# Another order of work in the cached attention stage of a four-part block

## The reference, cut to what matters

```
h = layernorm(x)
q, k_new, v_new = h @ wq.T, h @ wk.T, h @ wv.T
k = concat(k_cache, k_new);  v = concat(v_cache, v_new)      # 1601 cached + 256 new keys
x = x + (softmax(q @ k.T / 16) @ v) @ wo.T
```

## Time and profile before

| | |
|---|---|
| median of three runs | 1695.53 us |
| the profiled execution, its own time | 1699.32 us |
| its span, first to last instruction | 1697.5 us |
| PE busy over the span | 1455.1 us (86%) |
| DVE, ACT, POOL busy over the span | 1160.9, 984.3, 568.0 us |
| mean granted PE clock over the span | 0.94 |
| cached attention: first to last instruction | 0 to 199.13 us |
| PE busy in 0 to 199.2 us | 143.88 us (granted clock 0.89) |
| DVE, ACT, POOL busy in it | 90.08, 83.19, 49.76 us |

### The profile page before, as it was taken

One profiled execution on the slowest core, in us unless ns is written; L12 is line 12 of the kernel. 1 busy time (PEld: TensorE's weight loads), 2 busy tenths in 40 slices (PEclk: granted clock), 3 DMA queues, 4 the chain that ended last, 5 costly groups with the idle time before them and its releaser, 6 DMA issues. The chain is left out here.

```text
span 1697.5 us, 27527 instructions
## 1 busy us (share of the span) xinstructions
PE 1455.1 (86%) x10079; PEld 1363.0 (80%) x10082; DVE 1160.9 (68%) x2329; ACT 984.3 (58%) x2062; POOL 568.0 (33%) x470
## 2 busy tenths in 40 slices
PE   5778547888858989899999989999989999999945
PEld 4677546877747989899999989999989999999823
DVE  4553466888856777667676766777766677777657
ACT  3445216787735656566666566665656656666535
POOL 2223313453244522343223343233324333322134
PEclk8988857999979999999999999999999999999968
DMA  5132118889812302011011110110201101000010
GB/s 190 64 115 102 35 60 278 293 292 321 269 56 53 80 4 68 20 39 41 7 41 44 31 50 9 40 41 8 68 20 38 42 8 41 20 8 23 26 50 25
DMA packets 83547, 128.05 MB, mean 75 GB/s; under 512 B 17108, under 2 KB 63352, under 8 KB 83032
## 3 DMA queue, kind: packets, MB, share of 16 engines
q1 hardware_dynamic: 78856, 113.84, 20.8%
q0 software_dynamic: 4560, 12.46, 2.8%
HBM read 114.28 MB, written 11.99 MB: 74 GB/s over the span
## 5 line engine op out<-in xcount | busy, mean ns | idle before, releaser
L1843 ACT ACTIVATE ga_pT<-ga_ps_t 128x512 fp32r<-128x512 f32 (+1 forms) x512 | 243.7, 516 | 255.0 <-PE ga_ps_t L2077 254.7
L1978 DVE TENSOR_TENSOR ga_pT<-ga_ps_t,ga_pT 128x512 fp32r<-128x512 f32 (+1 forms) x512 | 280.2, 583 | 95.7 <-ACT ga_pT L1843 93.6
L1851 ACT ACTIVATE ga_probs<-ga_ps_s,ga_neg_max 128x1200 f32<-128x1200 f32 (+1 forms) x256 | 235.5, 927 | 91.8 <-DVE ga_neg_max L1999 91.4
L2077 PE MATMUL ga_ps_t<-all_eye,ga_probs 128*128 128x128 f32 (+1 forms) x1664 | 227.0, 274 | 9.7 <-DVE ga_pT L1978 9.6
L2077 PEld LDWEIGHTS ga_ps_t<-all_eye,ga_probs 128*128 128x128 f32 (+1 forms) x1664 | 193.0, 141 | 19.6 <-DVE ga_pT L1978 12.4
L1994 DVE TENSOR_REDUCE ga_part_max<-ga_ps_s 128x1 f32<-128x1200 f32 x128 | 178.8, 1397 | 12.4 <-PE ga_ps_s L2028 11.1
L1745 POOL TENSOR_TENSOR ga_oT<-ga_out_n,ga_oT 128x256 fp32r<-128x256 f32 x64 | 47.5, 742 | 394.8 <-ACT ga_oT L1866 394.8
L2028 PE MATMUL ga_ps_m<-ga_pT,ga_v 128*128 128x256 f32 (+1 forms) x1248 | 174.1, 287 | 3.3 <-DVE ga_pT L1978 3.2
L2028 PE MATMUL ga_ps_m<-ga_pT,side_v 128*128 128x256 f32 (+1 forms) x1248 | 174.8, 287 | 0.5 <-DVE ga_pT L1978 0.3
L2028 PE MATMUL ga_ps_t<-side_w_kv,side_encT 128*128 128x256 f32 (+1 forms) x1170 | 162.2, 288 | 13.7 <-DVE ga_pT L1978 8.4
L2028 PEld LDWEIGHTS ga_ps_t<-side_w_kv,side_encT 128*128 128x128 f32 (+1 forms) x1170 | 144.8, 186 | 23.2 <-DVE ga_pT L1978 11.2
(11 more groups left out here) (293 smaller groups left out, 2649.3 us busy)
## 6 DMA issues: line engine op xcount, KB each, us to landing
ex_raw<-in_L_ffn_packed SPq DMA_DIRECT2D x63, 704.0 KB, 5.8
side_w_q_raw<-in_L_xattn_Wq SPq DMA_DIRECT2D x16, 512.0 KB, 4.9
side_w_q_raw<-in_L_xattn_Wo SPq DMA_DIRECT2D x16, 512.0 KB, 4.6
ga_inv_rows<-ga_inv_row SPq DMA_DIRECT2D x64, 128.0 KB, 3.0
mix_y_rows<-ex_y SPq DMA_DIRECT2D x63, 128.0 KB, 4.1
side_enc<-in_ctx_turned SPq DMA_DIRECT2D x12, 512.0 KB, 5.6
ca_keys<-in_ctx_turned SPq DMA_DIRECT2D x12, 464.0 KB, 6.7
ca_cache<-in_ctx SPq DMA_DIRECT2D x4, 1024.0 KB, 5.5
```

Source lines behind the costliest of these rows:

```text
L1843: nc.scalar.activation(dst(HI), src, ACT.Copy, scale=scale).then_inc(read, 1)
L1851: nc.scalar.activation(dst, src, ACT.Exp, bias=neg_max[:, n % 2:n % 2 + 1], accum_out=half_sum[:, n % 4, k:k + 1]).then_inc(exped, 1)
L1978: nc.vector.tensor_tensor(dst(LO), src, f32(dst(HI)), ALU.subtract).then_inc(empty, 1)
L2077: mm = nc.tensor.transpose(out[0:top, i * P:(i + 1) * P], probs[step % PB][:, tile * P:tile * P + top], eye[:, :])
```

## The change

Work of the cached attention is moved between steps; no arithmetic is added or removed. DRAIN goes from 3 to 4.

- xT of row b+1 goes from the odd step 2b+1 to the end of the even step 2b. The norm of row b+1 goes from the end of that even step to its head on DVE, ahead of `invert` and `largest`.
- v of row 0 goes from step 2 to step 0. The other v keep their step.
- y of row b-2 goes from the even step to the odd step after it (on PE behind the first two turns; `add` on DVE behind those turns).
- f and `ternary_scale` of matrix b-1 go from the even step to the end of the odd step; `ternary_sum` from the middle to the end of the even step on ACT; `ternary_sign` from the end of the odd step to the middle of the next even step.
- The cached values are split in three pieces of 4, 4 and 5 tiles, all three in the even step, on ACT and on POOL. The weigh pieces wait for the piece that they need.
- In the odd step, q stands between the first and the second `keys_high`. In the prologue ACT does xT ahead of the keys and the weights K ahead of the third piece of keys.
- On SP the next keys are issued ahead of the first half of the cached values.

```diff
-    halves = [range(0, 8), range(8, KT)]
+    thirds = [range(0, 4), range(4, 8), range(8, KT)]
...
         if t:
             to = b + 1
-            xT, q, k = ([(kind, 0, to)] if to < B else [] for kind in ("xT", "q", "k"))
-            return first + turns[0:2] + xT + values[0:1] + q + turns[2:3] + k + values[1:2] + turns[3:4]
-        v = [("v", 0, b - 1)] if 0 <= b - 1 < B else []
-        y = [("y", 0, b - 2)] if 0 <= b - 2 < B else []
-        f = [("f", 0, b - 1)] if 0 <= b - 1 < W else []
-        return first + turns[0:2] + values[0:1] + turns[2:3] + values[1:2] + turns[3:4] + v + y + f
+            q, k = ([(kind, 0, to)] if to < B else [] for kind in ("q", "k"))
+            y = [("y", 0, b - 2)] if 0 <= b - 2 < B else []
+            f = [("f", 0, b - 1)] if 0 <= b - 1 < W else []
+            return first + turns[0:2] + y + values[0:1] + q + turns[2:3] + k + values[1:2] + turns[3:4] + f
+        v = [("v", 0, row) for row in ((0,) if b == 0 else (b - 1,) if 1 <= b - 1 < B else ())]
+        xT = [("xT", 0, b + 1)] if b + 1 < B else []
+        return first + turns[0:2] + values[0:1] + turns[2:3] + values[1:2] + turns[3:4] + v + xT
...
@@ SyncE
             for b in range(1, B):
-                load_cache(b, 0)
                 if b + 1 < B:
                     load_keys(b + 1)
+                load_cache(b, 0)
                 load_cache(b, 1)
...
@@ GpSimd
-                if 0 <= b - 1 < B:
-                    split_cache(b - 1, t)
+                if t == 0 and 0 <= b - 1 < B:
+                    for h in range(3):
+                        split_cache(b - 1, h)
...
@@ ScalarE, prologue
             weight_high(Q)
+            ring(("xT", 0, 0))
             keys_high(0, 0)
             keys_high(0, 1)
-            ring(("xT", 0, 0))
+            weight_high(K)
             keys_high(0, 2)
+            ring(("q", 0, 0))
             keys_high(0, 3)
-            weight_high(K)
-            ring(("q", 0, 0))
             ring(("k", 0, 0))
...
@@ ScalarE, odd step
-                        ring(("xT", 0, to))
                         keys_high(to, 0)
+                        ring(("q", 0, to))
                         keys_high(to, 1)
-                        ring(("q", 0, to))
...
-                    if 0 <= b - 1 < B:
-                        cache_high(b - 1, 1)
-                    if 0 <= b - 1 < W:
-                        ternary_sign(b - 1)
@@ ScalarE, even step
                 else:
+                    if b == 0:
+                        ring(("v", 0, 0))
                     if 0 <= b - 1 < B:
                         cache_high(b - 1, 0)
-                    if 0 <= b - 1 < W:
-                        ternary_sum(b - 1)
                     for e in turns[2:3]:
                         ring(e)
                     if 0 <= b - 2 < B:
                         result_high(b - 2)
                     for e in turns[3:4]:
                         ring(e)
+                    if 0 <= b - 2 < W:
+                        ternary_sign(b - 2)
                     if 0 <= b - 1 < B:
+                        cache_high(b - 1, 1)
+                    if 1 <= b - 1 < B:
                         ring(("v", 0, b - 1))
+                    if b + 1 < B:
+                        ring(("xT", 0, b + 1))
+                    if 0 <= b - 1 < B:
+                        cache_high(b - 1, 2)
+                    if 0 <= b - 1 < W:
+                        ternary_sum(b - 1)
...
@@ VectorE
                 turns = turned_probs(n)
+                if t == 0 and b + 1 < B:
+                    norm(b + 1)
                 if t == 0 and 0 <= b - 1 < B:
                     invert(b - 1)
...
                 if t:
                     to = b + 1
+                    if 0 <= b - 2 < B:
+                        add(b - 2)
                     if to < B:
-                        ring(("xT", 0, to))
                         ring(("q", 0, to))
...
                     if to < B:
                         keys_low_part(to, 3)
+                    if 0 <= b - 1 < W:
+                        ternary_scale(b - 1)
                 else:
...
                     for e in turns[3:4]:
                         ring(e)
+                    if 1 <= b - 1 < B:
+                        ring(("v", 0, b - 1))
                     if b + 1 < B:
-                        norm(b + 1)
-                    if 0 <= b - 1 < B:
-                        ring(("v", 0, b - 1))
-                    if 0 <= b - 2 < B:
-                        add(b - 2)
-                    if 0 <= b - 1 < W:
-                        ternary_scale(b - 1)
+                        ring(("xT", 0, b + 1))
```

More of the change, by code:

```diff
@@ L82, in cached_attention @@
     N = B * QT
-    DRAIN = 3
+    DRAIN = 4
     TB = 3
@@ L267, in load_cache @@
                 if b:
-                    sp.wait_ge(v_lo, 2 * (b - 1) + h + 1)
+                    sp.wait_ge(v_lo, 3 * (b - 1) + h + 2)
                 if h == 0:
@@ L329, in split_cache @@
             def split_cache(b, h):
-                at = slice(halves[h][0], halves[h][-1] + 1)
-                pool.wait_ge(v_hi, 2 * b + h + 1)
+                at = slice(thirds[h][0], thirds[h][-1] + 1)
+                pool.wait_ge(v_hi, 3 * b + h + 1)
                 nc.gpsimd.tensor_tensor(v[:, LO, at, :], cache[:, at, :], f32(v[:, HI, at, :]), ALU.subtract
@@ L359, in cache_high @@
             def cache_high(b, h):
-                at = slice(halves[h][0], halves[h][-1] + 1)
-                act.wait_ge(cache_in[h], (16, 32)[h] * (b + 1))
+                at = slice(thirds[h][0], thirds[h][-1] + 1)
+                act.wait_ge(cache_in[h // 2], (16, 32)[h // 2] * (b + 1))
                 if b:
-                    act.wait_ge(weighed, 2 * (b - 1) + h + 1)
+                    act.wait_ge(weighed, 2 * (b - 1) + h // 2 + 1)
                 nc.scalar.activation(v[:, HI, at, :], cache[:, at, :], ACT.Copy).then_inc(v_hi, 1)
@@ L531, in _ @@
             ring(("xT", 0, 0))
+            weight_low(K)
             keys_low_part(0, 2)
+            ring(("q", 0, 0))
             keys_low_part(0, 3)
-            weight_low(K)
-            ring(("q", 0, 0))
             ring(("k", 0, 0))
@@ L562, in _ @@
                         keys_low_part(to, 3)
-                else:
+                    if 0 <= b - 1 < W:
+                        ternary_scale(b - 1)
+                else:
+                    if b == 0:
+                        ring(("v", 0, 0))
                     for e in turns[2:3]:
@@ L654, in weigh @@
                 if piece == 0:
-                    pe.wait_ge(v_lo, 2 * u + half + 1)
+                    pe.wait_ge(v_lo, 3 * u + 1 + 2 * half)
                     if half == 0 and u:
@@ L659, in weigh @@
                         pe.wait_ge(*emptied(("v", 0, u)))
+                if half == 0 and piece == 1:
+                    pe.wait_ge(v_lo, 3 * u + 2)
                 k = 2 * half + piece
```

## The result

| | before | after |
|---|---|---|
| median, us | 1695.31 (1694.84 to 1697.14, 4 runs) | 1651.41 (1648.91 to 1655.37, 4 runs) |
| ratio | | 0.9741, 95% interval 0.9721 to 0.9762 |
| profiled execution, its time and span | 1699.32, 1697.5 | 1655.37, 1653.6 |
| first scores of the stage | 17.39 | 17.60 |
| last `add` of the stage ends | 199.13 | 156.62 |

A forecast was written before the change was run, and what follows sets the result against it. PE's nine idle gaps and the low clock behind each were taken to bound the stage. Start 16.2, matmuls 119.8, waits 19.0 and low clock 8.3 gave 163.3 against 199.1 us, so 1660 in all; range 1645 to 1676.

The forecast's parts named there:

- Matmuls at full clock, 119.8 us: PE's unchanged work from the first scores on, summed from gap-free stretches: 119.8 us at full clock.
- First scores at 16.2: Prologue: the cached attention's first scores start at 16.2 us instead of 17.4; bounds 15 and 17.4.
- Waits, 19.0 us: PE's remaining waits in the stage: 2.1 + 4.3 + 1.9 + 0.7 + 2.5 + 1.75 + 0.9 + 2.4 + 2.4 us.
- the two behind the ternary load: q of step 5 waits 2.5 us, the third turn of step 7 1.75, for banks ACT frees late; bounds 0 and 6.5.
- Rival A: Ternary load lands in time and gaps of 2 to 2.5 us don't lower the clock: 1648 us; chance 0.15.
- Step 4: PE waits 0.7 us for xT's bank, held by the third turn: free at 14.0, PE there at 13.4.
- Low clock, 8.3 us: PE runs slow after each of four gaps over 2 us before the tail, 2.07 us each: 8.3 us.
- The nine gaps: PE's idle gaps of 2.9 to 5.5 us in the kernel before, each costing 2.07 us of low clock besides.
- Later stages only move: Stages after cached attention start their loads behind its last instruction, so they keep taking 1498.4 us.
- B: ACT's line decides: `ternary_sum` holds the next step's turns 4 us longer, twice, with low clock: 1672 us; chance 0.14.
- D: Slower: the norm ahead of `largest` waits behind POOL's key splits and delays the next scores: above 1699 us; chance 0.03.
- E: No change: the next stage gives the time back, 1695 us; chance 0.02.
- C: Four more small PE waits of 0.6 to 1.9 us each bring 2.07 us of low clock: 1668 us; chance 0.08.

The follow-up runs named there:

- second profile: The changed kernel run and profiled once more, unchanged: 0.9746 of the kernel before, stage end 159.65 us.
- better version: Changed kernel with y back in the even step and ACT's key HI parts, third turn and v moved earlier: 0.9679, again 0.9695 of the kernel before.
- undo_ternary: Changed kernel with ternary_sum, ternary_sign, f and ternary_scale back in their old places: 0.9781 of the kernel before, stage end 160.31 us.
- norm_behind_max: Changed kernel with the norm behind `largest` on DVE in the even step: 0.9752 of the kernel before, stage end 158.61 us.
- before_filled: Kernel before, with 36 unused identity transposes on PE at five waits of q and y: 0.9993 of the kernel before, stage end 201.07 us.

## Why the prediction was right, point by point

The forecast held: faster, by mechanism and place; the size was 18% short (35.8 for 43.9 us). The stage ended 6.7 us ahead of the 163.3 of the sum: the start cost 1.4 more, the waits 3.8 less, the low clock 4.2 less. In the second profile it was 3.7 us ahead.

- *Matmuls at full clock, 119.8 us*: in the second run of the better version PE is busy 120.5 us at a clock of 1.00. Right.
- *First scores at 16.2*: 17.60, 1.4 us short. ACT's copy of the weights K began at 13.17 and not 12.65: it waited for their load. More than that, k then took 2.93 us, not 1.65, which the sum did not have. In three other profiles with the same prologue (`undo_ternary`, `norm_behind_max`, the second of `better`) k took 1.64 to 1.68 behind the same wait of 1.7 us, and the scores began at 16.4 to 16.6. The q ahead of it took 2.90 in every kernel, so PE starts slow here and becomes fast before or after this k; the profile gives 1.00 as the granted clock of both, and does not show when.
- *Waits, 19.0 us*: 15.2. Those for `exp` in step 1 were 2.1 against 1.54, step 2's keys 3.7 against 3.64, the y of step 9 2.4 against 2.26, the tail 2.4 against 2.4. The mis-sized ones are the two behind the ternary load, 2.5 and 1.75 against 0.54 and 0.40: the load landed 2.2 us sooner than in the row that was used. The values' half was no longer ahead of it, and with the pieces alone it lands as soon (5.6 us). Rival A said so. Step 4 waits 2.2 instead of 0.7.
- *Low clock, 8.3 us*: 123.9 - 119.8 = 4.1 in the first profile, 7.2 in the second. This is the term that was furthest off. It had four gaps over 2 us ahead of the tail; there were two (3.64, 2.26), and only the first was followed by low clock. In the second profile there were three (2.10, 3.62, 2.26), all followed by it, and the price of 2.07 each is about right. Near 2.1 to 2.3 us the price is a matter of chance (below).
- *What removed which gap*: the sum did not need to know. The prediction saw in the pieces the end of the drain's waits and the shorter splits; undone and alone they are worth some 20 us, and alone they also take away the y gaps, by an earlier ternary load. y's new place is worth nothing that can be seen. The nine gaps were counted once each and all but a short wait for `exp` went, so the sum did not depend on who removed them.
- *The parts*: tokens 9.6 undone, 11.6 alone; pieces 19.8 and 21.5. They add up to 29 to 33 of 42.5 (30 to 38 of 43.9 by the ratios). The ternary order is worth 3.7 by the stage end. Some 6 to 9 us are left, perhaps to what the parts do for each other (the norm away from POOL's pieces, xT's bank away from `ternary_sum`), to the prologue, and to v of row 0; these were not tried alone.
- *Later stages only move*: they take 1490.7 to 1502.5 us over the kernels of the table, all with the same code there. Right, and wider than most of the effects above.
- The rivals: 1651.4 lies nearer to rival A (1648) than to the forecast (1660). Both of A's conditions came in the first profile: the load in time, and a wait of 2.26 us without low clock; the second of them did not come in the second profile. The range held A as well, and 1651.4 is in it with room on both sides. B, D and E did not happen. C did not: the waits of 1.4 to 1.5 us were followed by full clock.
- The port: hits did come that the sum left out, 2.56 us for `ca_bias`, which ends at 58.84 where POOL's last piece ends at 58.82. This agrees with the Trainium skill (SBUF — State Buffer, section "Who interferes with whom"), by which the shared ports are held for a whole instruction. PE had other work there and did not wait: its next gap is in step 4.

## What to carry to other kernels

Before a gap is priced by the work moved out of its way, follow the late input back to its DMA issue and ask what that issue stood behind: here a buffer freed earlier, and so a load issued 2.2 us earlier with nothing ahead of it, took away the gaps that two reorderings aimed at. Count the bottleneck's gaps once, whoever removes them, and count with each what follows it. Undo each part of a working change: one of the four here brought nothing that could be seen, and a version without it, with three more moves, was 9 us faster.

## What the runs showed of the hardware

The low clock follows a gap, and the length of the gap nearly decides it. Over all fourteen profiles, from the first scores to the end of the stage, PE's waits of 0.35 us and more divide like this, by the granted clock of the 3 us behind each:

| wait of PE | number | followed by low clock |
|---|---|---|
| 0.35 to 2.04 us | 75 | 1, within 1 us of a wait of 3.84 |
| 2.06 to 2.26 us | 8 | 5 |
| 2.30 us and more | 48 | 48 |

In between it is a matter of chance from one execution to the next: the same wait of y, 2.26 us, was followed by full clock in the first profile of the changed kernel (1.68 us for the 12 matmuls) and by 2.84 us in the second. The low clock need not begin at once. The 3.64 us ahead of step 2 were followed by 1 us at 1.00 and then 3.4 us at 0.51 in the first profile, by 0.50 from the start and for longer in the second. The scores of step 1 ran slow in the second profile alone, behind 2.10 us where the first has 1.54. Together these end the stage 3.0 us later with the same idle time. The rows of the second profile, and then the other 18 matmuls of the scores of step 2 in the first (its first six are shown above):

```profile
26.99 6.88 PE L593 MATMUL ca_ps_s<-ca_kT,ca_qT 128*128 128x464 f32 x24 [2.10 <-ACT ca_probs L379]
...
40.25 7.66 PE L593 MATMUL ca_ps_s<-ca_kT,ca_qT 128*128 128x464 f32 x24 [3.62 <-POOL ca_kT L327]
...
140.86 2.84 PE L593 MATMUL ca_ps_t<-ca_w,ca_oT 128*128 128x256 f32 x12 [2.26 <-DVE ca_v L486]
```
```profile
40.63 5.22 PE L593 MATMUL ca_ps_s<-ca_kT,ca_qT 128*128 128x464 f32 x18 [0.16 <-POOL ca_kT L327]
```

The transposes of the identity kept the clock up in the gap ahead of q: 36 of them, 4.1 us with nothing else on PE, and the clock was 1.00 over the 9.5 us behind (`before_filled`).

A DVE instruction on one column with two inputs in SBUF (`ca_bias`) is held by a POOL subtraction just as a wide one is: 2.56 us instead of 0.22.
